# Windowed attention in a fused kernel: attend moved behind the next tile's scores, and its neighbours' part done in padded passes

## What is computed

```python
xn = layernorm(x, ln_g, ln_b)
q, k, v = split(xn @ w_qkv, 3)            # 8 heads of 64
q, k, v = (towin(q), towin(k), towin(v))  # windows of 64 tokens
kk, vv = around(k), around(v)             # the window and its two neighbours: 192 keys
sim = einsum('bhnwd,bhnWd->bhnwW', q * DH ** -0.5, kk)   # ends of a sequence masked
o = einsum('bhnwW,bhnWd->bhnwd', softmax(sim), vv)
light = o @ w_out
```

## Time and profile before

| | |
|---|---|
| median of 3 runs | 5010.83 us (4998.68 to 5011.06) |
| the profiled execution | 4995.12 us, its span 4993.4 us |
| PE busy | 4441.7 us, 89% of the span, 38850 matmuls |
| DVE, ACT, POOL busy | 2838.6, 2062.2, 862.9 us |
| light stage, 720 to 3153 us | PE 2324.75 us busy, DVE 1283.20, ACT 1042.35, POOL 534.41, clock 0.98 |

### The profile page before, as it was taken

The page is one execution under the profiler, slowest core; times in us unless marked ns, Lnnn a source line. Parts: engine busy times, 40 slices in busy tenths (PEclk is TensorE's granted clock), DMA queues, the critical chain, the costliest instruction groups (busy, mean ns, idle before and its releaser), DMA issues. The chain is left out here.

```text
span 4993.4 us, 98959 instructions
## 1 busy us (share of the span) xinstructions
PE 4441.7 (89%) x38850; PEld 3582.8 (72%) x38850; DVE 2838.6 (57%) x5251; ACT 2062.2 (41%) x5308; POOL 862.9 (17%) x678
## 2 busy tenths in 40 slices
PE   6688739999999999999999999545999999999999
PEld 6677637777777777777777777434777777777776
DVE  5688735554554545555555553587546546546545
ACT  4444314444444444444444442413434434434434
POOL 0122201221221222222222222110011011011011
PEclk9999959999999999999999999556999999999999
DMA  6868641111111111111111100101012021021110
GB/s 216 237 176 227 163 137 37 46 41 44 44 43 45 45 40 46 46 40 46 40 46 46 46 31 31 46 0 43 14 45 44 14 48 40 17 48 26 32 39 12
DMA packets 302269, 302.35 MB, mean 61 GB/s; under 512 B 16752, under 2 KB 214640, under 8 KB 301808
## 3 DMA queue, kind: packets, MB, share of 16 engines
q1 hardware_dynamic: 223472, 228.78, 15.6%
q0 software_dynamic: 12288, 33.56, 3.2%
q10 hardware_dynamic: 66048, 33.56, 2.5%
HBM read 203.04 MB, written 76.02 MB: 56 GB/s over the span
## 5 line engine op out<-in xcount | busy, mean ns | idle before, releaser
L1199 POOL TENSOR_TENSOR l_prob<-l_prob,l_inv 128x768 f32<-128x768 f32 x256 | 370.9, 1470 | 1991.8 <-DVE l_inv L1168 1991.8
L999 ACT ACTIVATE l_prob<-l_ps_s,l_neg_max 128x192 f32<-128x192 f32 (+2 forms) x1152 | 462.1, 418 | 400.0 <-DVE l_neg_max L1147 399.2
L2052 DVE TENSOR_REDUCE h_neg_max<-h_ps_s 128x1 f32<-128x1024 f32 x256 | 313.3, 1224 | 201.6 <-PE h_ps_s L1839 199.5
L1973 ACT ACTIVATE h_prob<-h_ps_s,h_neg_max 128x1024 f32<-128x1024 f32 x256 | 285.9, 1117 | 343.1 <-DVE h_neg_max L2055 303.4
L1147 DVE TENSOR_REDUCE l_neg_max<-l_ps_s 128x4 f32<-128x768 f32 (+2 forms) x288 | 256.4, 923 | 86.2 <-PE l_ps_s L857 85.3
L671 PE MATMUL l_ps_b<-l_xt_hi,w_qkv_hi 128*128 128x512 f32 x640 | 271.2, 424 | 31.3 <-issue 30.0
L1851 PE MATMUL h_ps_t<-ident,h_prob 128*128 128x128 f32 x2048 | 277.4, 278 | 7.6 <-ACT h_prob L1973 7.6
L1863 PE MATMUL h_ps_o<-h_probs_t,h_val 128*64 128x128 f32 x4096 | 278.4, 279 | 0.0
L1863 PEld LDWEIGHTS h_ps_o<-h_probs_t,h_val 128*64 128x64 f32 x4096 | 218.5, 136 | 80.1 <-issue 52.9
L1021 ACT ACTIVATE l_at_hi<-l_ps_d 128x512 fp32r<-128x512 f32 x128 | 76.6, 598 | 467.5 <-PE l_ps_d L891 457.7
L1851 PEld LDWEIGHTS h_ps_t<-ident,h_prob 128*128 128x128 f32 x2048 | 222.6, 140 | 60.5 <-issue 42.9
(11 more groups left out here) (365 smaller groups left out, 11244.3 us busy)
## 6 DMA issues: line engine op xcount, KB each, us to landing
xin<-in_L_attn_x_dram SPq DMA_DIRECT2D x32, 1024.0 KB, 5.4
xg<-in_L_attn_x_dram SPq DMA_DIRECT2D x64, 512.0 KB, 9.2
toep_back<-taps_padded ACTq DMA_DIRECT2D x32, 1024.0 KB, 9.8
x<-xg SPq DMA_DIRECT2D x64, 512.0 KB, 9.6
l_xin<-x SPq DMA_DIRECT2D x128, 256.0 KB, 2.9
l_xres<-x SPq DMA_DIRECT2D x128, 256.0 KB, 2.9
out_dram<-l_res SPq DMA_DIRECT2D x128, 256.0 KB, 2.0
h_q_hi<-h_q_hi SPq DMA_DIRECT2D x64, 128.0 KB, 5.3
```

The costliest lines, as they stand in the source:

```text
L999: last = nc.scalar.activation(prob[t % 2][rows, h, pair, cols], ps_s[rows, h, pair, cols], ACT.Exp, bias=neg_max[rows, t % 2, h, pair:pair ...
L1199: nc.gpsimd.tensor_tensor(mine, mine, spread(inv[:, t % 2, h, :], [1, PAIRS], [0, WIN + P]), ALU.mult).then_inc(p_normed, 1)
L1973: nc.scalar.activation(prob[i % 2][:, :].rearrange("p (a k) -> p a k", a=2), ps_s[i % 2][:, :, :], ACT.Exp, bias=neg_max[:, qt % 2, h:h + ...
L2052: nc.vector.tensor_reduce(at, ps_s[i % 2][:, :, :].rearrange("p a k -> p (a k)"), AX_X, ALU.max, negate=True).then_inc(max_step, 1)
```

## The change

PE's step becomes: unit 1 (`ps_b`), output product of tile `g-10` (`ps_c`), unit 2 (`ps_a`), scores of tile `g-7`, attend of tile `g-9` (`ps_d`), side turns (`ps_c`) and main turns (`ps_b`, `ps_a`) of tile `g-8`, unit 3 (`ps_d`), turn of the next x (`ps_c`). The pipeline is one step longer. `attend` does the neighbours' part in eight passes of the main form: `pt_side` is widened to 128 queries and zeroed where a key's half doesn't reach a query's half, and `val_side` holds the values of the half tile behind (lower partitions) and of the half tile before (upper partitions), put there by two transfers of 128 KB within the SBUF. At the ends of a sequence a part of `pt_side` is zeroed instead. `before_made` and its wait go. `x2n` and `xn` have one buffer, and `layernorms` runs for tile `g+1`. ACT does the copy of unit 2 and `at_hi` ahead of the exponentials; DVE does `at_lo` and the side copies (two halves) ahead of the copy of the main turns.

The diff, cut to its core:

```diff
@@ tensors @@
-        x2n = sb("l_x2n", [P, 2, DIM])
-        xn = sb("l_xn", [P, 2, DIM])
+        x2n = sb("l_x2n", [P, DIM])
+        xn = sb("l_xn", [P, DIM])
+        val_side = sb("l_val_side", [P, 2, HDH])
-        pt_side = sb("l_pt_side", [P, 2, PAIRS, WIN])
+        pt_side = sb("l_pt_side", [P, 2, PAIRS, P])
@@ sync @@
+                    if live(10):
+                        wait(sp, res_made, g - 9)
+                        sp.dma_start(out_t[g - 10], res[:, j % 2, :]).then_inc(res_out[j % 2], 16)
+                    if live(8):
+                        at = (j - 8) % NCH
+                        sp.dma_start(xres[:, j % 2, :], x2_t[g - 8]).then_inc(xres_in[j % 2], 16)
...
+                        for keys, tile in ((LO, at if at == NCH - 1 else at + 1), (HI, at if at == 0 else at - 1)):
+                            sp.dma_start(val_side[keys, j % 2, :], val[keys, tile % RING, :]).then_inc(side_in[j % 2], 16)
@@ tensor @@
+                def attend(j):
+                    for keys, probs in ((val[:, j % RING], pt_main), (val_side[:, j % 2], pt_side)):
                         for n in range(HEADS):
+                            h, pair = n % 2, n // 2
+                            last = nc.tensor.matmul(ps_d[h * DH:(h + 1) * DH, pair * P:(pair + 1) * P],
+                                                    keys[:, n * DH:(n + 1) * DH], probs[:, h, pair, :],
...
                 def body(g, j, live):
                     if live(4):
+                        wait(pe, main0_kept, g - 8)
                         first_unit(g, j)
+                    if live(10):
+                        wait(pe, o_kept, g - 9)
+                        wait(pe, xt_kept, done(g + 1))
...
+                    if live(3):
+                        wait(pe, main1_kept, g - 8)
+                        wait(pe, xt_kept, done(g + 1))
+                        if live(7):
+                            scores_ready(g, j)
+                        unit(ps_a, units(j)[1], u2_made)
...
                     if live(7):
                         scores(j)
+                    if live(9):
...
+                        wait(pe, side_kept, g - 8)
+                        wait(pe, u3_kept, done(g - 3))
+                        wait(pe, side_in[(j - 9) % 2], (g - j) * 16 + 32 * ((j - 9) // 2 + 1))
+                        attend(t)
                     if live(8):
                         t = (j - 8) % NCH
                         wait(pe, p_normed, 2 * (g - 7))
+                        wait(pe, res_made, g - 9)
+                        turn_side(t)
+                        wait(pe, u1_kept, done(g - 3))
+                        turn_main(ps_b, t, 0, main0_made)
+                        wait(pe, u2_kept, done(g - 2))
+                        turn_main(ps_a, t, 1, main1_made)
                     if live(3):
+                        wait(pe, o_kept, g - 8)
+                        unit(ps_d, units(j)[2], u3_made)
+                    if live(-1):
                         wait(pe, side_kept, g - 7)
                         transpose_x(g + 1, j + 1)
@@ scalar @@
+                    if live(-1):
+                        layernorms(g + 1, (j + 1) % NCH, (g - j) + GT * ((j + 1) // GT + 1))
+                    if live(3):
+                        wait(act, u2_made, g - 2)
+                        if live(7) and (j + 1) % GT in (0, 3):
+                            wait(act, s_made, g - 6)
+                        keep_unit(ps_a, units(j)[1], u2_kept)
+                    if live(9):
+                        wait(act, o_made, g - 8)
...
                     if live(7):
                         exps(g, (j - 7) % NCH, 0)
@@ vector @@
+                def keep_side(j):
+                    for rows, at, cut in ((LO, slice(WIN, P), j == NCH - 1), (HI, slice(0, WIN), j == 0)):
+                        to = pt_side[rows, :, :, at]
+                        if cut:
+                            last = nc.vector.memset(to, 0.0)
+                        else:
+                            last = nc.vector.tensor_copy(to, ps_c[rows, :].rearrange("p (h a q) -> p h a q", h=2, q=WIN))
+                    last.then_inc(side_kept, 1)
...
+                    if live(9):
+                        wait(v, o_hi_kept, g - 8)
...
                     if live(8):
+                        wait(v, side_made, g - 7)
+                        keep_side((j - 8) % NCH)
                         wait(v, main0_made, g - 7)
...
```

More of the change, by code:

```diff
@@ L839, in first_unit @@
                 def first_unit(g, j):
-                    wait(pe, u3_kept, done(g - 3))
+                    if isinstance(g, int) and g < 12:
+                        wait(pe, u1_kept, g - 4)
                     unit(ps_b, units(j)[0], u1_made)
@@ L991, in _ @@
                 layernorms(0, 0, GT)
-                layernorms(1, 1, GT)
                 keep_xt(0, 0)
```

141 lines of the change are left out of this document (46 added, 95 removed).

## The result

The changed kernel takes 4861.97 us, the median of 4 runs (4861.50 to 4865.87), against 5009.38 (4998.68 to 5011.06, 4 runs) before: a ratio of 0.9713, 95% interval 0.9701 to 0.9725. The forecast was 4855 us, faster; it was right, 7 us from the median.

The account below looks back on a forecast made before the run. The prediction took TensorE (PE) to bound the light stage. Its terms, -132 + 11 - 27 + 17 - 15 + 4 = -142 us, took the profiled 4995 us to 4853; it forecast 4855 us, range 4815 to 4915 for 8 in 10.

Parts of the forecast that it names:

- The step: PE's full step in the light stage falls from 18.05 to 17.02 us, 1.03 less; 128 steps give -132 us.
- Rival 2: Gaps in PE's step belong to waits, not tile shape, and stay: +65 us, 4920; chance 0.10.
- Waits that go, -27: PE's waits for the result's copy (16.8 us) and the main turns' copy (10.5 us) both go.
- (a): Unit 3's wait for at_hi and at_lo: ready 3.4 us after the scores, against 3.71 when main turns end.
- (b): One step in four, query unit's copy is ready 2.8 us after scores; main turns need it at 2.84.
- rival 1: at_hi or the query unit's copy comes 0.6 us later, PE waits in some 120 steps: +40, 4895; chance 0.18.
- The idle time at the back edge stays as it is: PE's idle time at the jump of the loop over sequences, 5.93 us once in each, does not change.
- Ends of the stage, -15: Steps after the last unit fall from 13.18 to 9.1 us; in all -15 us, bounds -25 and 0.
- Start, +4: One buffer for normalised x and two more buffers cleared at the start cost +4 us, bounds 0 and +8.
- the rest of the program, 0: Outside the light stage, where the changed code does not run, the sum has no term.
- rival 3: PE's clock falls in the 5.3 us run without a full product, up to 5530 us, slower; chance 0.04.
- rival 4: New stalls, from transfers or DVE's queue, eat 1 us a step; time stays within 15 us; chance 0.04.

Follow-up runs that it names:

- e10: e2 with TensorE's wait for its own passes put back between attend's main and side passes; 4981.08 us, 0.9953 of the kernel before.
- e1: The changed kernel with the old unpadded attend put back, so the new order alone; 4934.14 us, 0.9848 of the kernel before.
- e2: The kernel before with the padded attend, its transfers and one buffer of normed rows, in the old order; 4965.34 us, 0.9911 of before.
- e4: The changed kernel with the waits ahead of the scores moved from ahead of unit 2 to its last quarter; 4837.72 us, 0.9659 of before.
- e11: The changed kernel with VectorE's two routing dots moved behind the next step's copy of unit 1; 4836.46 us, 0.9663 of before.
- e3: The changed kernel with 16 more unread side turns ahead of the jump in each iteration's last step; 4896.10 us, one run.
- e9: The kernel before with one buffer of normed rows instead of two and nothing else; 5012.83 us, 1.0015 of before.
- e6: The changed kernel without the transfers of neighbours' values after the first two tiles, old values read; 4865.76 us, 0.9716 of before.
- e5: The changed kernel with GpSimd dividing only the side part of the probabilities, the main part left undivided; 4843.96 us, 0.9672 of before.

## Why the prediction was right, and where its terms were not

- **The step: right.** -1.03 us was forecast, 17.02 measured against 18.05; every part is within 0.03 of its term. The sum holds with a price for each change of tile shape read from the gaps in the earlier trace rows, and with 0.11 for a padded pair. Rival 2, that the gaps stay, is out. No run changes the tile shape and nothing else; the wait for its own passes, which went together with the gaps inside attend, has by e10 0.28 us of the 1.03. The rule weighed against it in the prediction (the Trainium skill, TensorEngine Tiling (Array Packing), Overview: a contraction of 64 is better packed in row tiles) doesn't hold for this kernel: in e10, where the padding comes without the loss of the wait, a plain step takes 17.68 us instead of 18.05. In e1 the old attend stands in the new order, and plain steps take 17.7 to 17.8 instead of 16.9 to 17.0.
- **Waits that go, -27: right in kind.** Both are gone from the view of waits. With the padding alone they grow by 19 us (e2).
- **New waits, (a) and (b): right.** In the step above attend follows the scores at 1954.95. `at_lo`, from the timeline of DVE in the same step:

```profile
1957.60 0.69 DVE L1168 TENSOR_TENSOR l_at_lo<-l_ps_d,l_at_hi 128x512 fp32r<-128x512 f32 x1 [0.71 <-ACT l_at_hi L1016]
```

  It ends 3.34 after the scores, and unit 3 starts 3.68 after them: 3.4 (with 0.14 to reach PE) against 3.71 was forecast. In plain steps PE waits for neither, so rival 1 is out. In the last tile of a sequence PE waits 1.4 (1.5 forecast), in the first up to 0.6 (0.6); over the stage 10.0 + 2.8 us, where +17 was forecast.
- **New waits, the missing one: wrong by +24 to +31.** The step that failed is the list of new waits: it went through the banks that unit 3 and the main turns need, counted from the end of the scores, and did not look at `scores_ready`, which the change moves ahead of unit 2. e4, which changes only that, gains 24 us of median and 31 of stage. Its deeper cause, that the dots fall beside GpSimd's division and take 1.47 instead of 0.98 us, could be read off neither engine's list alone; the prediction priced the instructions that move on DVE and not the ones they then run beside. e11 shows that cause, and the ends of the dots beside the division (above) show how.
- **"The idle time at the back edge stays as it is": wrong by -32.** It was taken as a property of the loop. e3 shows that it depends on what stands last ahead of the jump.
- **Ends of the stage, -15: right.** -18.2; a step of the drain takes 9.30 us (9.1 forecast) where it took 13.18, from the starts of the output product in the drain of the changed kernel:

```profile
2964.77 0.47 PE L671 MATMUL l_ps_c<-w_out_hi,l_at_hi 128*128 128x512 f32 x1 [0.86 <-DVE l_pt_side L1141]
...
2974.07 0.47 PE L671 MATMUL l_ps_c<-w_out_hi,l_at_hi 128*128 128x512 f32 x1 [0.86 <-DVE l_pt_side L1141]
```

- **Start, +4: right; the rest of the program, 0: wrong by +21 and +7.** What one buffer of normed rows costs lies in the first step behind the first turn of x: 28.92 us instead of 25.58, and 29.12 in e9, which has this part alone. But the light stage also starts 21 us later. It isn't the two clears that the change adds, since e1 has them and starts at 720.0. The time is lost in the convolution, which the change doesn't touch: matmul for matmul PE is 0.2 us later at 154 us and 20 us later at 561. ACT waits there longer for a transfer. Waits of ACT up to 745 us, before, changed and e9:

```profile
ACT toep L466 <- DMA toep_back<-taps_padded: 34.8, 13, 6.5
```

```profile
ACT toep L466 <- DMA toep_back<-taps_padded: 112.0, 22, 10.2
```

```profile
ACT toep L466 <- DMA toep_back<-taps_padded: 91.3, 21, 7.4
```

  That wait is not the cause, though: e9 has 91.3 us of it and starts the light stage at 721.6, while e4 has 75.6 and starts it latest of all, at 744.4. It isn't scatter of one profile: in the profiles of the three kernels with the unpadded attend (before, e1, e9) the first turn of x comes at 720.0 to 721.6, in those of the eleven with the padded one (the changed kernel and the other ten) at 737.1 to 744.4. e6, without most of the transfers, and e3, with more matmuls, have it too, and e1 has the transfers, the copies and the buffers without it. So neither the transfers nor the buffers cause it; it goes with the padded passes, or with the 1792 matmul records fewer that they bring, in a way that no run here shows. No run tried to take it away, and the +7 behind the light stage were not followed.
- **The clock (rival 3) and no effect (rival 4): out.** The granted clock is 1.00 in the stretch above and the run of short passes lasts 5.3 us at full speed. The Trainium skill, TensorE: Matmul & The Clock Gate, Part 4, has it that transposes don't count as activity for the clock. The prediction took that for a forecast that the clock falls here, and it isn't quite one: of the 5.3 us only the main turns, 0.85 us, are transposes, and scores, attend and side turns are plain matmuls. No run here tests a longer run of transposes in this stage.

Summed by these terms: -142 as forecast, +28 for the missing wait, -32 at the jumps, +21 and +7 outside the stage and -3 at the ends give -121, against -129.3 in span. Of the remaining -8 the two foreseen waits make up 4 (12.8 us for 17); the others lie within the stage and were not followed. The two errors that cost time and the one that saved it are what luck there was. Without the 32 us at the jumps, which nobody forecast, the kernel would have taken some 4894 us, still inside the range.

## What to carry to other kernels

When an instruction moves, go through everything that waits around its new place, also waits that only stand in front of it for the sake of something later; a wait belongs right ahead of what needs it (24 us here for four lines). What stands last ahead of a loop's jump decides how much of the jump is seen: put long passes there, not short ones. And judge a half of a change by its own stage as well as by the whole time, since 20 us moved in a stage that no edit touched.

## What the runs showed of the hardware

- A product of two SBUF inputs on DVE takes 0.69 us alone. Started while GpSimd is at work on SBUF it ends 0.54 to 0.55 us after that GpSimd instruction (677 of 677 dots in the kernels before, changed, e5 and e11), and takes up to 1.83; the GpSimd instruction that starts behind it waits in turn (1.89 us instead of 1.47). A transfer of 128 KB between partitions beside both changes neither (e6).
- 16 more short fp32 passes (32 records, 1.1 us) ahead of the loop's jump raise PE's idle time there from 1.6 to 3.4 us in the mean, and the jump's whole cost from 1.9 to about 5.7 us an iteration, and the granted clock of the 4 us behind is 0.50 to 0.69 (e3).
- After 5.5 to 6.5 us of idling PE came back at 1.2 GHz at all five jumps (before), after 1.4 to 1.8 us at 2.4 (changed), after 2.2 to 2.6 us at either (e2).
- A wait of PE for its own last pass, in the middle of a run, costs 0.28 us (e10 against e2).
- In the eleven profiles with the padded attend a stage that ended before it is 17 to 24 us longer than in the three without; unexplained.
